# The third layer's norm and mask in one run behind the statistics, its convolution from half slot 38

## The reference

```
x = x + L0(_gn(x))     # whitening: a 128 x 128 matrix per batch
x = x + L1(_gn(x))     # deformable sampling with 16 groups and 9 taps
x = x + L2(_gn(x))     # attention in 7 x 7 windows and between windows
x = x + L3(_gn(x))     # masked 3 x 3 convolution
```

```
m = 1 - (abs(posX - mu_x) + abs(posY - mu_y)) * mask_weight    # one mu per image and channel
m = maximum(m, -1.0);  m = where(filt == 1.0, m, 1.0)
out = conv3x3(maximum(x * m, 0.0), weight) + bias
```

## Time and profile before

| | us |
|---|---|
| three runs | 9752.37, 9764.28, 9761.67; median 9761.67 |
| profiled execution, its own time | 9744.27 |
| its span, first to last instruction | 9741.9 |
| TensorE matmuls busy | 8017.8 (82%) |
| VectorE busy | 7470.9 (77%) |
| ScalarE busy | 3944.2 (40%) |
| TensorE's mean granted clock | 0.91 of full |

### The profile page before, as it was taken

The page is one execution under the profiler, slowest core; times in us unless marked ns, Lnnn a source line. Parts: engine busy times, 40 slices in busy tenths (PEclk is TensorE's granted clock), DMA queues, the critical chain, the costliest instruction groups (busy, mean ns, idle before and its releaser), DMA issues.

```text
span 9741.9 us, 288919 instructions
## 1 busy us (share of the span) xinstructions
PE 8017.8 (82%) x123582; PEld 4494.0 (46%) x123582; DVE 7470.9 (77%) x9137; ACT 3944.2 (40%) x6124; POOL 191.2 (2%) x253
## 2 busy tenths in 40 slices
PE   6457888887888888788888878888887888888797
PEld 5424445454444545444454544445454444545454
DVE  2478778878787887878788687878878787886863
ACT  0034435353453535445353534435353443535432
POOL 0000000000000000000000000000000000000000
PEclk7579899998999999899999989999998999999998
DMA  5000201111020111102011110201111020111101
GB/s 117 0 20 20 56 26 49 32 45 44 25 58 26 50 32 45 45 26 57 26 50 32 46 43 28 58 24 49 32 45 44 27 60 24 48 32 46 43 25 55
DMA packets 231836, 391.50 MB, mean 40 GB/s; under 512 B 26736, under 2 KB 168016, under 8 KB 223312
## 3 DMA queue, kind: packets, MB, share of 16 engines
q1 hardware_dynamic: 230544, 372.67, 13.6%
HBM read 190.38 MB, written 130.55 MB: 33 GB/s over the span
## 4 chain that ended last, share of the span: by engine, by line
PE 58%; DVE 23%; issue 12%; ACT 6%; DVEq 1%; DMA 0%; SPq 0%; POOL 0%; ACTq 0%; POOLq 0%
PE ps L897 11%; PE ps L696 8%; PE ps L762 7%; DVE arena L1722 5%; PE ps L997 4%; PE ps L795 4%; PE ps L987 3%; PE ps L811 3%; DVE arena L1777 3%; PE ps L770 3%; PE ps L784 2%; PE ps L718 2%; DVE arena L1699 2%; DVE arena L1705 2%; DVE arena L1817 2%
## 5 line engine op out<-in xcount | busy, mean ns | idle before, releaser
L897 PE MATMUL ps<-arena,ident 64*64 64x512 f32 x5600 | 1748.1, 678 | 575.8 <-DVE arena L1722 575.6
L899 PE MATMUL ps<-arena,ident 48*64 48x512 f32 x5600 | 1751.6, 678 | 0.0
L1722 DVE TENSOR_TENSOR arena<-arena 112x2560 f32<-112x2560 f32 x560 | 1577.7, 2820 | 178.9 <-PE ps L899 173.4
L897 PEld LDWEIGHTS ps<-arena,ident 64*64 64x64 f32 x5600 | 485.9, 148 | 1600.0 <-issue 1591.3
L762 PE MATMUL ps<-arena,wqk 128*128 128x400 f32 x2048 | 884.0, 549 | 157.7 <-DVE arena L1826 115.2
L696 PE MATMUL ps<-vp,convw 128*128 128x448 f32 x2016 | 821.8, 549 | 13.5 <-ACT vp L1318 13.5
L1705 DVE TENSOR_TENSOR arena<-arena 112x576 f32<-112x576 f32 x1008 | 764.1, 758 | 34.9
L1239 ACT ACTIVATE arena<-ps 112x864 f32<-112x864 f32 x224 | 199.2, 889 | 1367.3 <-PE ps L718 1362.5
L811 PE MATMUL ps<-arena 64*64 64x33 f32 x32768 | 636.1, 225 | 121.2 <-issue 65.2
L1817 DVE TENSOR_REDUCE arena<-ps 128x16 f32<-128x800 f32 x512 | 505.3, 987 | 243.3 <-PE ps L784 239.3
L1811 DVE COPY arena<-ps 128x400 f32<-128x400 f32 x512 | 293.1, 572 | 515.4 <-PE ps L762 515.2
(11 more groups left out here) (300 smaller groups left out, 12520.5 us busy)
## 6 DMA issues: line engine op xcount, KB each, us to landing
windows_out<-arena SPq DMA_DIRECT2D x1024, 100.0 KB
arena<-windows_out SPq DMA_DIRECT2D x224, 256.0 KB, 3.9
arena<-windows_out SPq DMA_DIRECT2D x224, 192.0 KB, 3.3
arena<-in_wqk SPq DMA_DIRECT2D x16, 2048.0 KB, 7.9
arena<-in_x_t SPq DMA_DIRECT2D x16, 1568.0 KB, 10.5
arena<-in_x SPq DMA_DIRECT2D x16, 1568.0 KB, 7.2
arena<-arena SPq DMA_DIRECT2D x32, 784.0 KB
out_x<-xb SPq DMA_DIRECT2D x112, 224.0 KB, 2.2
```

Source lines behind the costliest of these rows:

```text
L897: nc.tensor.matmul(ps[half, 3, :], ident[0:SLOT, 0:SLOT], prod[0:SLOT, ring(c, dy), dx, :], start=(s < 2), stop=(s >= TAPS - 2), skip_grou ...
L899: mm = nc.tensor.matmul(ps[half, 4, :], ident[SLOT:PT, SLOT:], prod[SLOT:PT, ring(c, dy), dx, :], start=(s < 2), stop=(s >= TAPS - 2), ski ...
L1722: V.tensor_tensor(prod[0:PT, ring(c, dy), :, :].rearrange("p k (n e) -> p k n e", e=CG), taps.to_broadcast([PT, SHIFTS, N64, CG]), for_tap ...
```

## The change

It has four parts.

1. The steps of the third norm and of the mask vectors, in slots 38, 39 and 40 before, all stand in slot 37.
2. The outer sum, one VectorE instruction of 3136 elements before, becomes 56 ScalarE activations of one row (56 elements) each, whose bias is the row's mask value. They stand by chunks of 8 rows in slots 37, 37, 39, 40, 42, 44 and 47. Mask times image and relu go by chunks too, in slots 38, 38, 40, 42, 44, 47 and 50.
3. The convolution's pieces move from slots 44 to 64 to slots 38, 38, 39 to 45, 47, 49 and on to 64, and the last to `last_tiles` as before; the additions follow four slots after each chunk.
4. In the sampling's own work `sum_mask` and `norm_mask` stand in front of slot 2s of dy 3 (behind slot 2s + 1 before), and `rows_by_mask` in dy 4, behind M(s), in place of dy 3.

```diff
--- before.py
+++ after.py
@@ -53,11 +53,13 @@
 
 TOK_Q, TURN_Q, Q2_Q, S2_Q, SOFT_Q, A2_Q, AGG_Q = 2, 6, (8, 10), 12, 15, 18, 20
 GN_Q = AGG_Q + 17
-CONV_Q = [GN_Q + 7 + j for j in range(3 * CHUNKS)]
+CONV_Q = [38, 38, 39, 40, 41, 42, 43, 44, 45, 47, 49, 50, 51, 53, 54, 56, 58, 60, 62, 64, 2 * TR * SHIFTS - 2]
 ADD_Q = [at + 4 for at in CONV_Q[2:-1:3]] + [2 * TR * SHIFTS - 1]
+MASK_Q = [GN_Q, GN_Q, 39, 40, 42, 44, 47]
+MASKED_Q = [38, 38, 40, 42, 44, 47, 50]
 DVE_A, DVE_COV, DVE_POW = 20, 12, 22
 ACT_MAIN = 14
-DVE_PRE, DVE_MAIN, DVE_BLK, DVE_END = 6 + 8 * DW_BLOCKS, 105, 69, 63
+DVE_PRE, DVE_MAIN, DVE_BLK, DVE_END = 6 + 8 * DW_BLOCKS, 105, 69, 61
 
 
 
@@ -357,7 +359,8 @@
         ag_p, ag_s = sig("agg_psum", HALVES), sig("agg_sbuf", HALVES)
         y2_p, y2_s = sig("y2_psum", WS), sig("y2_added", WS)
 
-        v3_s, mk_s, rl_s = sig("v3"), sig("masked"), sig("relu", CHUNKS)
+        v3_s, ax_s, mm_s, mk_s, rl_s = sig("v3"), sig("mask_axes"), sig("mask_rows", CHUNKS), sig("masked", CHUNKS), sig(
+            "relu", CHUNKS)
         c3_p, c3_s = sig("conv_psum", CHUNKS), sig("conv_added", CHUNKS)
 
         block = ctx.enter_context(nc.Block())
@@ -961,14 +964,15 @@
                         aggregate(i, h)
                 elif q == GN_Q:
                     group_mean(i, 2, 2)
-                elif q in CONV_Q:
-                    k, dy = CONV_Q.index(q) // 3, CONV_Q.index(q) % 3
-                    if dy == 0:
-                        pe.wait_ge(rl_s.sem, rl_s.at(i, min(k + 2, CHUNKS)))
-                        pe.wait_ge(c3_s.sem, c3_s.at(i, max(k - 2, 0)))
-                    mm = conv_taps(k, k % 3, convw, range(3 * dy, 3 * dy + 3))
-                    if dy == 2:
-                        mm.then_inc(c3_p.sem, 1)
+                for piece in range(3 * CHUNKS):
+                    if CONV_Q[piece] == q:
+                        k, dy = piece // 3, piece % 3
+                        if dy == 0:
+                            pe.wait_ge(rl_s.sem, rl_s.at(i, min(k + 2, CHUNKS)))
+                            pe.wait_ge(c3_s.sem, c3_s.at(i, max(k - 2, 0)))
+                        mm = conv_taps(k, k % 3, convw, range(3 * dy, 3 * dy + 3))
+                        if dy == 2:
+                            mm.then_inc(c3_p.sem, 1)
 
             def aggregate(i, h):
                 nb, (first, count) = h // 2, half_tokens(h)
@@ -1305,18 +1309,23 @@
                     act.wait_ge(a2_p.sem, a2_p.at(i))
                     nc.scalar.activation(at2.rearrange("p (a n) -> p a n", a=2), ps[:, 0:2, :], ACT.Copy
                                          ).then_inc(a2_t.sem, 1)
-                elif q == GN_Q + 1:
+                elif q == GN_Q:
                     group_sqrt(i, 2)
-                elif q == GN_Q + 3:
                     act.wait_ge(gn_ab[2].sem, gn_ab[2].at(i))
                     nc.scalar.activation(vp_in, xb_yx, ACT.Identity, bias=sm[:, 29:30], scale=sm[:, 28:29]
                                          ).then_inc(v3_s.sem, 1)
-                elif q == GN_Q + 6:
-                    act.wait_ge(mk_s.sem, mk_s.at(i))
-                    for k in range(CHUNKS):
+                    act.wait_ge(ax_s.sem, ax_s.at(i))
+                for k in range(CHUNKS):
+                    if MASK_Q[k] == q:
+                        for h in range(k * ROWS, (k + 1) * ROWS):
+                            ins = nc.scalar.activation(mk[:, h, :], axy[:, W:], ACT.Identity, bias=axy[:, h:h + 1])
+                        ins.then_inc(mm_s.sem, 1)
+                for k in range(CHUNKS):
+                    if MASKED_Q[k] == q:
                         rows = slice(k * ROWS, (k + 1) * ROWS)
+                        act.wait_ge(mk_s.sem, mk_s.at(i, k + 1))
                         nc.scalar.activation(vp_in[:, rows, :], mk[:, rows, :], ACT.Relu).then_inc(rl_s.sem, 1)
-                elif 0 < q - AGG_Q < 2 * WS and (q - AGG_Q) % 2:
+                if 0 < q - AGG_Q < 2 * WS and (q - AGG_Q) % 2:
                     aggregated(i, q - AGG_Q - 1)
                     aggregated(i, q - AGG_Q)
 
@@ -1930,11 +1939,9 @@
                     if nb == WS - 1:
                         owne.settle()
                         group_stats(owne, i, 2)
-                elif q == GN_Q + 1:
+                elif q == GN_Q:
                     group_variance(owne, i, 2, 2)
-                elif q == GN_Q + 2:
                     group_scale(owne, i, 2)
-                elif q == GN_Q + 3:
                     dve.wait_ge(gn_ab[2].sem, gn_ab[2].at(i))
                     owne.step(V.tensor_scalar(sm[:, 35:36], sm[:, 29:30], float(W), None, ALU.mult))
                     owne.step(V.tensor_scalar(rsum, rsum, sm[:, 28:29], sm[:, 35:36], ALU.mult, ALU.add))
@@ -1956,16 +1963,16 @@
                     owne.step(V.tensor_scalar(axy[:, W:], pos, sm[:, 33:34], None, ALU.subtract))
                     owne.step(V.scalar_tensor_tensor(axy, axy, -1.0, axy, ALU.mult, ALU.max))
                     V.tensor_scalar(axy[:, 0:W], axy[:, 0:W], neg_mw, 1.0, ALU.mult, ALU.add)
-                    owne.mark(V.tensor_scalar(axy[:, W:], axy[:, W:], neg_mw, None, ALU.mult))
-                elif q == GN_Q + 4:
-                    owne.settle()
-                    owne.mark(V.tensor_tensor(mk, axy[:, 0:W].rearrange("p (n a) -> p n a", a=1).to_broadcast([C, H, W]),
-                                              axy[:, W:].rearrange("p (a n) -> p a n", a=1).to_broadcast([C, H, W]), ALU.add))
-                elif q == GN_Q + 5:
-                    owne.settle()
-                    dve.wait_ge(v3_s.sem, v3_s.at(i))
-                    V.scalar_tensor_tensor(mk, mk, floor1, vp_in, ALU.max, ALU.mult).then_inc(mk_s.sem, 1)
-                elif q in ADD_Q:
+                    V.tensor_scalar(axy[:, W:], axy[:, W:], neg_mw, None, ALU.mult).then_inc(ax_s.sem, 1)
+                for k in range(CHUNKS):
+                    if MASKED_Q[k] == q:
+                        rows = slice(k * ROWS, (k + 1) * ROWS)
+                        if k == 0:
+                            dve.wait_ge(v3_s.sem, v3_s.at(i))
+                        dve.wait_ge(mm_s.sem, mm_s.at(i, k + 1))
+                        V.scalar_tensor_tensor(mk[:, rows, :], mk[:, rows, :], floor1, vp_in[:, rows, :], ALU.max, ALU.mult
+                                               ).then_inc(mk_s.sem, 1)
+                if q in ADD_Q:
                     k = ADD_Q.index(q)
                     dve.wait_ge(c3_p.sem, c3_p.at(i, k + 1))
                     xk = xb[:, k * CH:(k + 1) * CH]
@@ -1983,6 +1990,9 @@
                             by_row(n, c, 1 if c else 2)
                         elif c and dy == 1:
                             by_row(n, c, 2)
+                        if ahead and dy == 3:
+                            sum_mask(n, c + 1)
+                            norm_mask(n, c + 1)
                         if i is not None:
                             after_windows(i, 2 * s)
                         if ahead and dy == 1:
@@ -1996,11 +2006,8 @@
                             far_flag(n)
                         if i is not None:
                             after_windows(i, 2 * s + 1)
-                        if ahead and dy == 3:
-                            sum_mask(n, c + 1)
-                            norm_mask(n, c + 1)
+                        if ahead and dy == 4:
                             rows_by_mask(n, c + 1)
-                        elif ahead and dy == 4:
                             by_row(n, c + 1, 0)
 
             def rest(i):
```

## The result

The changed kernel takes 9442.54 us, the median of four runs (9413.79 to 9447.01). The kernel before takes 9762.67 beside them. The ratio is 0.9672, with an interval of 0.9659 to 0.9686: 3.3% less. A second set of five runs, on another occasion, gave 9451.06 us and 0.9691 (0.9677 to 0.9705).

A forecast was written before the change was run, and what follows sets the result against it. VectorE and TensorE bound the sampling in turn. 21 us a pass over 15 passes plus 3.4 us in the last image take 9744.3 to 9425.9; 17.4 more for the median gives 9443 us; range 9400 to 9570.

The forecast's parts named there:

- Part 1: Norm and mask vector steps all in slot 37: M(19) starts 1.0 us later, TensorE's wait for it near 8.3 us.
- Part 2: Outer sum on ScalarE: VectorE gains net 2.6 us; rows 0.2 us each, 11.2 us a pass; relu 2 0.5 us late.
- Part 3: Convolution from slot 38: 19.0 us of waits and slow stretches dropped between S(19) and S(34), net 17.0 us a pass.
- Part 4: Softmax steps moved in the sampling: M(9) comes 4.4 us sooner, and 4.0 us a pass are kept.
- M(10) allows some 4: At S(10), which could start 4.4 us sooner: the multiply M(10) permits some 4 us of it.
- The last image: Image 15's rest: the convolution starts about 9685.9 in place of 9689.31, when relus 0 and 1 are done; 3.4 us.
- The sum: Whole kernel: 21 us a pass, 315 us over 15 passes; forecast 9443 us, 3.3% less.
- A sign that missed: TensorE's idle time in front of the successors of `multiply` L1722 down from 38 to about 15 us a pass.
- ScalarE is late: Rival: 8 us of ScalarE's added work lie on the path, a pass gives 13 us, time 9563 us; chance 0.12.
- VectorE is not the bound: Rival that VectorE's list is the bound after all: 11 us a pass, little from part 4, 9594 us; chance 0.10.
- TensorE's clock: Rival: TensorE, fed step by step, keeps falling to 1.2 GHz; with 60 us at that level 9897 us; chance 0.03.
- Nothing else ends the pass: Rival of no change: the pass ends on something else, such as the next image's load; chance 0.02.

The follow-up runs named there:

- all of part 4 undone: The changed kernel with the softmax sum, norm and rows-by-mask steps back in their old places: 9552.7 us, ratio 0.9785 to the kernel before.
- the forecast that missed by most: The changed kernel with mask vectors and the first two chunks' rows in slot 38, behind M(19), first relus in slot 39: forecast 9430 us, measured 9512.51 us.
- the projection's move: The changed kernel with ScalarE's relus ahead of mask rows, plus TensorE's projection of dy 4 ahead of `sum_taps`: 9406.5 us, ratio 0.9647 to the kernel before.
- that run: The changed kernel with one idle single-element ScalarE activation ahead of each of the 56 mask rows: 9491.28 us, ratio 0.9728 to the kernel before.
- part 4 alone: The kernel before with only the softmax sum and norm ahead of slot 2s and rows by mask in dy 4: 9673.39 us, ratio 0.9906.

## Why the prediction was right

**What bounds.** Right. TensorE's waits were the price. Putting the convolution back behind them costs 11.6 us a pass, while its work stays the same.

**Part 1.** M(19) was to be 1.0 us later, with a wait of 8.3 us at S(19). The wait is 8.25. `sum_mask` and `norm_mask` did fall into VectorE's wait in step 18; with all of part 4 undone, that cover and `rows_by_mask` behind M(19), S(19) was 4.4 us later and all of it was lost.

**Part 2.** The mask rows were sized at 0.2 us each from the nearest row, an activation from PSUM; they take 0.23 (56 in 13.1 us). The estimate of 0.23 us from the page "ScalarE: Activation LUTs" of the Trainium skill, section "What ACT_TABLE_LOAD costs", was the closer one, and the trace agrees with it. It made no difference: relus 0 and 1 still came before TensorE asked, and relu 2 was 0.57 us late against my 0.5. The other rule of that page of the Trainium skill, in its section "Rules for kernel authors", additions on VectorE, would have cost 1.9 to 2.6 us a pass here, since VectorE was waited for and ScalarE was not. It holds for the move in one block and started late, which was slower than the kernel before. A wait that I had not named came up, 3.01 us on VectorE for the exponential of step 23 (1310.02 in its timeline); it lies inside VectorE's lead and TensorE never sees it.

**Part 3.** I took 19.0 us of waits and slow stretches away and gave 1.0 back. From S(19) to S(34) the pass shown went from 127.8 to 109.2 us, 18.6 less where the sum had 18.0: 14.9 of it are waits (15.9 to 1.0) and 3.7 are matmuls at the higher clock in place of the lower. The sum put all of it down to the convolution's place. The runs divide the 19.7 us gained between M(19) and M(34): with the convolution back in its slots 8.1 stay gained, because VectorE's list ahead of M(21) and M(22) is shorter, and the place itself is worth 11.6. TensorE and VectorE did follow each other closely at the end without a wait of more than 0.3 us.

**Part 4.** I had 4.0 us; from M(0) to M(10) VectorE gained 2.7, and up to S(19) some 3 remain when the 1.0 us of part 1 is taken out. This term was too large, and the step that had it wrong is "M(10) allows some 4": M(10) came only 2.7 us sooner. In the pass shown TensorE's S(10) waits 2.67 us for it, so VectorE leads there and not TensorE; over the 15 passes it waits 1.1 us on average.

```profile
1130.40 0.61 PE L900 MATMUL ps<-arena,ident 64*64 64x512 f32 x1 [1.60 <-DVE arena L1731]
...
1165.37 0.61 PE L900 MATMUL ps<-arena,ident 64*64 64x512 f32 x1 [2.93 <-DVE arena L1731]
...
1176.68 0.61 PE L900 MATMUL ps<-arena,ident 64*64 64x512 f32 x1 [2.67 <-DVE arena L1731]
```

The waits at S(4), S(9) and S(10) are 1.60, 2.93 and 2.67 us, where S(4) and S(9) had 3.35 and 5.50.

**The last image.** The convolution starts 10.58 us behind the copy of the means (9391.42 - 9380.84), where it was 13.45: 2.9 us gained against 3.4. It then lasts 50.17 us in place of 49.47, so some 2.2 us are left at its end.

```profile
9380.84 0.16 DVE L1560 COPY sm<-ps 128x2 f32<-128x2 f32 x1 [0.68 <-PE ps L670]
```

```profile
9391.42 50.17 PE L699 MATMUL ps<-vp,convw 128*128 128x448 f32 x126 [10.62 <-ACT vp L1327]
```

**The sum.** 21 us a pass was forecast and 21.8 came between M(0) and M(34); the attention, longer by chance, took some back. Two terms miss by 1 us each and cancel. On average S(19) came 2.0 us sooner where the terms gave 3.0, and S(19) to S(34) gained 19.0 where they gave 18.0. That the median fell within a microsecond of 9443 is luck beyond what the terms deserve: two sets of the same kernel differ by 9 us.

**A sign that missed.** TensorE's idle time for `multiply` was to fall from 38 to about 15 us a pass. It fell to 23. The forecast's own terms take away 14.9 us behind S(19), 1.9 at S(4) and about 2.5 at S(9), and add 1.0 at S(19), which leaves 20 and not 15 (an estimate from them). The waits that it did not name, at S(8) and S(10), are 1.0 and 1.1 us on average.

**The rivals.** ScalarE is late only at the margin: 10 us more of work on it cost 3.7. VectorE is not the bound, though it is within 6 us of it in 109. TensorE's clock rose to 0.98 in the stretch, where its idle time is 1.0 us in place of 15.9. Nothing else ends the pass: from M(34) to the next w0s it takes 15.9 us, and 15.5 before.

## What to carry to other kernels

Where two engines lead in turn, look for work of the one that may run early enough to lie in its waits for the other: here 50 us of convolution, its cost unchanged, began 5 us behind S(19) in place of 40, and 11.6 us a pass hung on that, more than on any work taken away. Such a move needs its inputs early, and in pieces: the same outer sum on ScalarE was worth a gain by chunks and started early, and a loss in one block and started late. Before a step is moved, walk the queue of each engine on its path and name what stands ahead of it there, for the forecast that missed by most, 82 us, had left out a copy that waited for something else. And where a move helps in one step of a loop, look at the other steps that it changes: the projection's move gained 1.8 us behind S(19) and lost 1.4 at S(10).

## What the runs showed of the hardware

A ScalarE activation of 56 elements per partition with a bias column, from SBUF, lasts 0.33 us and the next starts 0.23 us after it. One of a single element lasts 0.28 us, and the row behind it starts 0.19 us later (1266.24 and 1266.43 in that run). So some 0.2 us of such a row are fixed, and for rows this short their number, more than their length, makes the cost.

Whether TensorE falls to the lower of its two clock levels behind a wait of about 3 us is not told by the wait's length. A sum's first matmul takes 0.61 us at the higher level and 1.08 at the lower. Behind the waits of 5.13 to 12.65 us shown above S began at the lower level. With part 4 alone S(19) waits 2.97 us and begins at the lower level in all 15 passes; S took 5.3 us there in place of 2.7. S(21) with the convolution back in its old slots does so behind 2.87 us, too. S(9) of the changed kernel waits 2.93 to 3.23 us and begins at the lower level in 6 passes of 15. S(10) in the version with the projection ahead waits 4.38 us in every pass. Its first matmul runs at the higher level in about half of them, and within the sum the clock falls in these as well.
